# Attention back stage: a step's small products moved from its end to mid-step

## The chip, the cores and the metric

The kernel runs on one core of one Trainium2 chip. The metric is the device time of one execution in microseconds. Three runs of the kernel before gave 2210.7, 2211.61 and 2214.48 us; the median is 2211.61 us.

## What is computed

The input x is 16 batches of 512 tokens of 128 values in f32. The reference chains six blocks:

```python
x = x + 0.5 * _L0_ffn_ref(_layernorm(x), ...)   # 16 experts, top 2, and a shared one
x = x + _L0_attn_ref(_layernorm(x), ...)         # linear attention
x = x + 0.5 * _L0_ffn_ref(_layernorm(x), ...)
x = x + 0.5 * _L1_ffn_ref(_layernorm(x), ...)    # relu MLP of width 512
x = x + _L1_attn_ref(_layernorm(x), ...)         # softmax attention, 16 heads of 8
x = x + 0.5 * _L1_ffn_ref(_layernorm(x), ...)
```

The last two are the part of this case:

```python
# _L1_attn_ref
xn = _layernorm(x, ln_scale, ln_bias)
q, k, v = xn @ wq, xn @ wk, xn @ wv              # each split into 16 heads of 8
scores = jnp.einsum('bhid,bhjd->bhij', q, k)
probs = jax.nn.softmax(scores / jnp.sqrt(128.0), axis=-1)
out = jnp.einsum('bhij,bhjd->bhid', probs, v)    # heads joined again
return out + xn
# _L1_ffn_ref
h = jax.nn.relu(x @ w1 + b1)
return h @ w2 + b2
```

## The kernel before

The program has two stages, one after the other. The front (`build_front`) does the first four blocks and writes its result to the DRAM tensor `mid`. The back (`build_back`, from L882) does the last two. The change touches the back alone. In the notes below PE is the matrix engine, DVE the vector engine, ACT the scalar engine, POOL and SP the two others.

**Batches and steps.** The back has 16 batches. A batch has 16 steps k: 4 groups g of 4 heads, and in each group 4 blocks of 128 keys (`STEPS = GRP * T`). Every engine runs its own `batch_steps(B)` once for each batch, with its own written order of instructions; semaphores tie the orders together. The program is written out for batches -2 to 16, and what does not exist is left out.

**What a step does.** A step has four units j, one for each head of the group.
- `scores` (L1404) writes the transposed scores of a key block and 512 queries, 128x512, into an ST bank. ACT takes the exponential (L1184) into `pr`. Below such a tile is called ST0 to ST3.
- `first_scores` (L1417) writes 128 queries by 512 keys into an MX bank, 7 steps ahead (`AHEAD`). DVE takes the maximum of each row (L1302) into `nm`. These are MX0 to MX3. After four steps the maxima of a group are transposed (`nm`, L1379), copied with the sign changed by ACT (L1168), and sent by SP (L1049) into an extra row of `qt`, from where they shift the scores.
- `weighted` (L1432) multiplies the exponentials of the step before with the values into the bank PV. It waits for all four exponentials of that step (L1425). It is called PV below.

**The order on PE in a step** (L1436 to L1447) is ST0, MX0, ST1, MX1, PV of the step before, ST2, MX2, ST3, MX3, and at the end the small products of that step. The scores use 32 rows of the array each, and the four units sit on four different groups of rows.

**Small products.** The table `SMALL` (L856) gives each step its list. Its names: `xt` transposes the normalised input of the next batch; `kp`, `qp` and `v` are the projections to keys, queries and values; `nm` the transposed maxima; `ot` the transposed output of a group; `ft` transposes the input of the MLP; `g` are four products into the hidden layer, and `y` its two output products. Three engines follow the list:
- PE makes the product into a bank.
- ACT handles `v` and `g` and `nm` (`FOR_ACT` and `nm`). For `xt`, `kp`, `qp`, `ft` (`BY_BOTH`) ACT copies the high part and then DVE subtracts it for the low part (L1230 to L1239).
- DVE handles `ot` and `y`.

**Rings.** PSUM has 8 banks: 3 for ST, 4 for MX, one for PV. `ST_RING` and `MX_RING` (L871 to L877) list all that goes into these banks in PE's order; an entry's place modulo the number of banks is its bank. `v` and `g` are in the ST ring, all others in the MX ring. `wait_bank` (L1335) makes PE wait until the entry that had the bank before has been used. The ST ring has 69 places, the MX ring 78, and both start anew with every batch.

**Orders of the others.** ACT: exponentials 0 and 1, then every fourth step the copy of PV (L1190), exponentials 2 and 3, then the small ones. DVE: maximum 0, then the low parts of the step before, maximum 1, then `side` (statistics of the layer norms), maxima 2 and 3, then `ot` and `y`. SP issues the transfers in the order of L1052 to L1074, POOL the normalisations in the order of L1105 to L1133. They wait on the semaphores `khi_ready`, `used["kp"]`, `used["nm"]`, `used["ot"]`, `used["y"]` and the like.

Of the kernel before, what the change touches and what calls it, by code (L numbers as in the profile page):

```python
# [36 lines left out]
HG = H // GRP  # L37
# [69 lines left out]
def build_front(nc, weights, x_dram, mid_dram, ident_dram, turns):  # L107
# [748 lines left out]
SMALL = [  # L856
# [4 lines left out]
FOR_ACT = ("v", "g")  # L861
BY_BOTH = ("xt", "kp", "qp", "ft")
# [3 lines left out]
def ahead_of(k):  # L866

    return (0, k + AHEAD) if k + AHEAD < STEPS else (1, k + AHEAD - STEPS)


ST_RING, MX_RING = [], []  # L871
for _k, _small in enumerate(SMALL):
    _rel, _s = ahead_of(_k)
    ST_RING += [("st", 0, _k * HG + _j) for _j in range(HG)] + [one for one in _small if one[0] in FOR_ACT]
    MX_RING += [("mx", _rel, _s * HG + _j) for _j in range(HG)] + [one for one in _small if one[0] not in FOR_ACT]
ST_PLACE = {one: _p for _p, one in enumerate(ST_RING)}
MX_PLACE = {one: _p for _p, one in enumerate(MX_RING)}  # L877

# [3 lines left out]
def build_back(nc, weights, mid_dram, out_dram, staged_dram, tail_dram, batches):  # L882
    w = weights
    with ExitStack() as ctx:
# [97 lines left out]
        def first_head(u):  # L982

            return (u + HG // 2) % HG
# [5 lines left out]
        def bank_of(name, rel, n):  # L990
            if name in FOR_ACT:
                return ST[ST_PLACE[name, rel, n] % ST_BANKS]
            return MX[MX_PLACE[name, rel, n] % MX_BANKS]

        def program(batch_steps):


            for n in range(-2, batches + 1):
                batch_steps(Batch(n // 2, n % 2))
# [143 lines left out]
        @block.scalar  # L1143
        def _(act):
            def small(B, rel, name, n):
                C = B + rel
                if not C.exists or name not in IN_ACT:
                    return
                p = C.parity
                act.wait_ge(made[name].sem, C.at(made[name], n + 1))  # L1150
                m = bank_of(name, rel, n)
                if name == "xt":
                    nc.scalar.activation(xh[:], m[:], ACT.Copy).then_inc(xh_ready.sem, 1)
                elif name == "kp":
                    if not C.first:
                        act.wait_ge(staged.sem, C.at(staged, 0))
                    nc.scalar.activation(khi[:], m[:], ACT.Copy).then_inc(khi_ready.sem, 1)
                elif name == "qp":
                    if not C.first:
                        act.wait_ge(staged.sem, C.at(staged, 0))  # L1160
                    nc.scalar.activation(qhi[:], m[:], ACT.Copy).then_inc(qhi_ready.sem, 1)
                elif name == "ft":
                    nc.scalar.activation(fh[:], m[:], ACT.Copy).then_inc(fh_ready.sem, 1)
                elif name == "nm":
                    if n >= 2 or not C.first:
                        before = (C, n - 2) if n >= 2 else (C + -1, n + GRP - 2)
                        act.wait_ge(shift_in[before[1]].sem, before[0].at(shift_in[before[1]], 16 * T))
                    nc.scalar.activation(nr[n % 2][:], m[0:32, 0], ACT.Copy, scale=-1.0).then_inc(used["nm"].sem, 1)  # L1168
                elif name == "v":
                    nc.scalar.activation(va[p][:, :, :, 0:DH], m[:].rearrange("p t (h e) -> p t h e", h=H),  # L1170
                                         ACT.Copy).then_inc(used["v"].sem, 1)
                elif name == "g":
                    nc.scalar.activation(hid[n][:], m[:], ACT.Relu, bias=w["b1"][:, n:n + 1]).then_inc(used["g"].sem, 1)

            def exponential(B, k, j):
                if not B.exists:
                    return
                u = k * HG + j
                act.wait_ge(made["st"].sem, B.at(made["st"], u + 1))
                if j == 0 and (k >= 2 or not B.first):  # L1180

                    act.wait_ge(pv_mm.sem, B.at(pv_mm, k - 1))
                bank = ST[ST_PLACE["st", 0, u] % ST_BANKS]
                nc.scalar.activation(pr[k % 2][:, j], bank[:].rearrange("p a b -> p (a b)"),  # L1184
                                     ACT.Exp, scale=SM_SCALE).then_inc(used["st"].sem, 1)

            def weights_out(B, g):
                if B.exists:
                    act.wait_ge(pv_mm.sem, B.at(pv_mm, T * (g + 1)))
                    nc.scalar.activation(oTs[g % 2][:], PV[:], ACT.Copy).then_inc(pv_out.sem, 1)  # L1190

            def batch_steps(B):
                for k in range(STEPS):
                    for j in range(HG):
                        exponential(B, k, j)
                        if j == 1 and k == 0:
                            weights_out(B + -1, GRP - 1)
                        elif j == 1 and k % T == 0:
                            weights_out(B, k // T - 1)
                    for name, rel, n in SMALL[k]:  # L1200
                        small(B, rel, name, n)

            program(batch_steps)

        @block.vector
        def _(dve):
# [83 lines left out]
            def maximum(B, rel, u):  # L1290

                C = B + rel
                if not C.exists:
                    return
                g, t, j = u // (HG * T), u // HG % T, first_head(u)
                dve.wait_ge(made["mx"].sem, C.at(made["mx"], u + 1))
                if u % (HG * T) == 0 and (g >= 2 or not C.first):
                    before = (C, g - 1) if g >= 2 else (C + -1, g + GRP - 1)
                    dve.wait_ge(made["nm"].sem, before[0].at(made["nm"], before[1]))
                c = t * HG + j  # L1300
                bank = MX[MX_PLACE["mx", rel, u] % MX_BANKS]
                nc.vector.tensor_reduce(nm[g % 2][:, c:c + 1], bank[:].rearrange("p a b -> p (a b)"), AX.X,  # L1302
                                        ALU.max).then_inc(used["mx"].sem, 1)

            def batch_steps(B):
                for k in range(STEPS):
                    rel, s = ahead_of(k)
                    maximum(B, rel, s * HG)
                    for name, r, n in SMALL[k - 1]:
                        if name in BY_BOTH:  # L1310
                            small(B, r, name, n)
                    maximum(B, rel, s * HG + 1)
                    side(B, k)
                    maximum(B, rel, s * HG + 2)
                    maximum(B, rel, s * HG + 3)
                    for name, r, n in SMALL[k]:
                        if name not in IN_ACT:
                            small(B, r, name, n)

            for k in range(2):  # L1320
                own.step(nc.vector.memset(nm[k][:], 0.0))
            own.settle()
            program(batch_steps)

        @block.tensor
        def _(pe):
# [68 lines left out]
            def scores(B, k, j):  # L1395

                if not B.exists:
                    return
                g, u = k // T, k * HG + j
                if k % T == 0 and j == 0:  # L1400
                    pe.wait_ge(shift_in[g].sem, B.at(shift_in[g], 16 * T))
                place = ST_PLACE["st", 0, u]
                wait_bank(B, ST_RING, ST_BANKS, place)
                pe.matmul(flat(ST[place % ST_BANKS]), kt_[g][rows_of(j), k % T], flat(qt[g])[rows_of(j)], start=True,  # L1404
                          stop=True).then_inc(made["st"].sem, 1)
# [30 lines left out]
            def batch_steps(B):  # L1436
                for k in range(STEPS):
                    rel, s = ahead_of(k)
                    for j in range(HG):
                        scores(B, k, j)  # L1440
                        first_scores(B, rel, s * HG + j)
                        if j == 1 and k == 0:
                            weighted(B + -1, STEPS - 1)
                        elif j == 1:
                            weighted(B, k - 1)
                    for name, r, n in SMALL[k]:
                        small(B, r, name, n)  # L1447

            program(batch_steps)

# [254 lines left out]
```

## Time and profile before

| | |
|---|---|
| median of three runs | 2211.61 us |
| profiled execution, device time | 2212.05 us |
| its span | 2210.3 us |
| mean granted clock of PE | 0.969 |
| busy in the span: PE | 1984.1 us (90%) |
| DVE | 1650.0 us (75%) |
| ACT | 1083.3 us (49%) |
| POOL | 585.6 us (26%) |

The profiled execution stands 0.44 us from the median. In the page's view of 40 slices the back begins at about slice 24 and fills the rest. The engine PEld in the rows is the loading of weights into PE, which overlaps its products. Ends of matmuls are modelled, so the starts are what is read. In the timeline view instructions of one kind that follow each other are merged, with their number after x; the time given is from the first start to the last end. Four score products of different row groups run side by side, so that four starts lie within 0.01 us.

### The profile page before, as it was taken

Reading aid. Unit: us, or ns where it says so; the run is one execution under the profiler, and the core shown is the slowest. Engines: PE = TensorE matmul, PEld = TensorE weight load, DVE = VectorE, ACT = ScalarE, POOL = GpSimd, SP = SyncE. Lnnn points to the kernel's source line nnn. Section 1 sums busy time; section 2 is a strip of 40 time slices with the busy share of each in tenths; the row PEclk is TensorE's granted clock in tenths of the full one; section 3 lists DMA queues with packets and bytes.
Section 4 is the critical chain, followed back from the end, with each engine's and each line's share of the span. In section 5 each row is a group of like instructions: output and inputs, shape, how many; then the busy total and the mean of one; then the engine's idle time right before and its main releaser. Section 6 shows DMA issues by size and latency. Waiting matters only on the chain. (4 is left out here: it accounts for less than half of the span.)

```text
span 2210.3 us, 34280 instructions
## 1 busy us (share of the span) xinstructions
PE 1984.1 (90%) x12468; PEld 1352.9 (61%) x12468; DVE 1650.0 (75%) x4096; ACT 1083.3 (49%) x1971; POOL 585.6 (26%) x621
## 2 busy tenths in 40 slices
PE   3998999899989998989899838999999999999997
PEld 3787778777877787778777723344444444444444
DVE  5766776767676767776767518988988888889982
ACT  3333323332333233323332214777777777777775
POOL 3332333233223331333133021222222222222211
PEclk9999999999999999999999956999999999999999
DMA  3000000000000000000000022222222222222220
GB/s 119 6 11 10 1 11 10 11 1 10 11 10 1 10 11 10 1 11 11 10 1 6 5 72 81 73 81 84 78 78 78 78 87 88 78 78 78 73 73 10
DMA packets 49991, 85.81 MB, mean 39 GB/s; under 512 B 6752, under 2 KB 11104, under 8 KB 49760
## 3 DMA queue, kind: packets, MB, share of 16 engines
q1 hardware_dynamic: 47920, 81.85, 11.6%
q8 instruction: 99, 1.62, 0.3%
q10 hardware_dynamic: 1904, 1.78, 0.2%
q14 instruction: 68, 0.56, 0.1%
HBM read 49.26 MB, written 34.87 MB: 38 GB/s over the span
## 5 line engine op out<-in xcount | busy, mean ns | idle before, releaser
L1302 DVE TENSOR_REDUCE b_nm<-b_MX 128x1 f32<-128x512 f32 x1024 | 651.8, 683 | 80.1 <-PE b_MX L1417 71.4
L1184 ACT ACTIVATE b_pr<-b_ST 128x512 f32<-128x512 f32 x1024 | 551.7, 601 | 175.8 <-PE b_ST L1404 173.9
L383 ACT ACTIVATE s<-G 128x512 f32<-128x512 f32 x306 | 182.9, 598 | 432.3 <-PE G L685 423.2
L1417 PE MATMUL b_MX<-b_kt,b_qt 32*128 32x512 f32 x1024 | 357.7, 505 | 20.8 <-DMA b_qt<-staging 8.3
L690 PE MATMUL Y<-w_wd,h 128*128 128x128 f32 x2448 | 335.0, 281 | 8.6 <-DVE h L544 8.0
L690 PEld LDWEIGHTS Y<-w_wd,h 128*128 128x128 f32 x2448 | 315.0, 195 | 23.9 <-DVE h L544 13.4
L1404 PE MATMUL b_ST<-b_qt,b_kt 32*128 32x512 f32 x1024 | 305.8, 497 | 19.5 <-ACT b_pr L1184 18.7
L1404 PEld LDWEIGHTS b_ST<-b_qt,b_kt 32*128 32x128 f32 x1024 | 123.3, 183 | 317.0 <-ACT b_pr L1184 214.4
L535 DVE TENSOR_TENSOR su<-U,s 128x512 f32<-128x512 f32 x272 | 186.3, 685 | 160.8 <-ACT s L383 83.1
L1432 PE MATMUL b_PV<-b_pr,b_va 128*32 128x512 f32 x2048 | 276.2, 612 | 0.0
L544 DVE TENSOR_TENSOR h<-C,su 128x512 f32<-128x512 f32 x272 | 188.1, 692 | 9.3
L1417 PEld LDWEIGHTS b_MX<-b_kt,b_qt 32*128 32x128 f32 x1024 | 142.9, 186 | 60.7 <-DVE b_nm L1302 34.0
L683 PE MATMUL U<-xh,w_wuh 128*128 128x512 f32 x306 | 128.3, 419 | 57.6 <-DVE su L535 44.0
L305 POOL TENSOR_TENSOR vpe_s<-mv_s,w_eps 128x4 f32<-128x4 f32 x33 | 6.6, 199 | 627.0 <-DVE mv_s L437 627.0
L683 PE MATMUL G<-xh,w_wgh 128*128 128x512 f32 x306 | 145.6, 476 | 0.0
L1098 POOL TENSOR_TENSOR b_ve<-b_mv,w_eps_two 128x4 f32<-128x4 f32 x16 | 3.2, 201 | 445.9 <-DVE b_mv L1219 445.9
L685 PE MATMUL G<-xl,w_wgh 128*128 128x512 f32 x306 | 121.3, 396 | 0.0
L685 PE MATMUL U<-xl,w_wuh 128*128 128x512 f32 x306 | 121.2, 396 | 0.0
L684 PE MATMUL G<-xh,w_wgl 128*128 128x512 f32 x306 | 120.9, 395 | 0.0
L684 PE MATMUL U<-xh,w_wul 128*128 128x512 f32 x306 | 120.8, 395 | 0.0
L683 PEld LDWEIGHTS U<-xh,w_wuh 128*128 128x128 f32 x306 | 57.7, 189 | 97.0 <-DVE su L535 58.8
L718 PE MATMUL C<-cT,w_pairs 128*128 128x512 f32 x272 | 109.1, 401 | 0.0
(237 smaller groups left out, 3431.9 us busy)
## 6 DMA issues: line engine op xcount, KB each, us to landing
b_kt<-staging SPq DMA_DIRECT2D x64, 256.0 KB, 2.8
b_qt<-staging SPq DMA_DIRECT2D x64, 256.0 KB, 3.1
staging<-b_khi SPq DMA_DIRECT2D x32, 256.0 KB, 3.0
staging<-b_qhi SPq DMA_DIRECT2D x32, 256.0 KB, 3.0
xin<-in_x SPq DMA_DIRECT2D x17, 256.0 KB, 2.6
mid<-xo SPq DMA_DIRECT2D x17, 256.0 KB, 2.0
b_x<-mid SPq DMA_DIRECT2D x16, 256.0 KB, 2.9
staging<-b_klo SPq DMA_DIRECT2D x16, 256.0 KB, 3.1
```

What stands on the lines that cost most here:

```text
L383: nc.scalar.activation(sbuf_s[n % 2][:], G[n % 2][:], ACT.Silu).then_inc(act_done.sem, 1)
L535: nc.vector.tensor_tensor(out[:], U[:], sbuf_s[n % 2][:], ALU.mult).then_inc(up_used.sem, 1)
L544: nc.vector.tensor_tensor(h[n % 3][:], C[:], su[n % 2][:], ALU.mult).then_inc(h_ready.sem, 1)
L683: pe.matmul(flat(bank), wh, flat(high), start=True, stop=False)
L684: pe.matmul(flat(bank), wl, flat(high), start=False, stop=False)
L685: return pe.matmul(flat(bank), wh, flat(low), start=False, stop=True)
L690: mm = pe.matmul(bank[:, t], hid[:, t], wd, start=(first and t == 0), stop=True, skip_group_check=True)
L1184: nc.scalar.activation(pr[k % 2][:, j], bank[:].rearrange("p a b -> p (a b)"), ACT.Exp, scale=SM_SCALE).then_inc(used["st"].sem, 1)
L1302: nc.vector.tensor_reduce(nm[g % 2][:, c:c + 1], bank[:].rearrange("p a b -> p (a b)"), AX.X, ALU.max).then_inc(used["mx"].sem, 1)
L1404: pe.matmul(flat(ST[place % ST_BANKS]), kt_[g][rows_of(j), k % T], flat(qt[g])[rows_of(j)], start=True, stop=True).then_inc(made["st"].sem, 1)
L1417: pe.matmul(flat(MX[place % MX_BANKS]), qt[g][rows_of(j), u // HG % T], flat(kt_[g])[rows_of(j)], start=True, stop=True).then_inc(made["mx ...
L1432: mm = pe.matmul(flat(PV)[rows_of(j)], va[B.parity][:, kt, g * HG + j], pr[k % 2][:, j], start=(kt == 0), stop=(kt == T - 1), skip_group_c ...
```

## The change

In the two rings, the small products of a step get their places after unit 1 and before unit 2 (before: after unit 3). PE issues them directly behind PV, between unit 1 and unit 2. ACT handles its own after exponential 1 (and the copy of PV, where there is one). DVE does `ot` and `y` between `side` and maximum 2, and the low parts of the same step between maximum 2 and maximum 3 (before: in the next step, after maximum 0). SP's and POOL's programs are unchanged.

```diff
 for _k, _small in enumerate(SMALL):
     _rel, _s = ahead_of(_k)
-    ST_RING += [("st", 0, _k * HG + _j) for _j in range(HG)] + [one for one in _small if one[0] in FOR_ACT]
-    MX_RING += [("mx", _rel, _s * HG + _j) for _j in range(HG)] + [one for one in _small if one[0] not in FOR_ACT]
+    for _half in (range(0, 2), range(2, HG)):
+        ST_RING += [("st", 0, _k * HG + _j) for _j in _half]
+        MX_RING += [("mx", _rel, _s * HG + _j) for _j in _half]
+        if 0 in _half:
+            ST_RING += [one for one in _small if one[0] in FOR_ACT]
+            MX_RING += [one for one in _small if one[0] not in FOR_ACT]
...
 # ACT, batch_steps
-                    for name, rel, n in SMALL[k]:
-                        small(B, rel, name, n)
+                        if j == 1:
+                            for name, rel, n in SMALL[k]:
+                                small(B, rel, name, n)
...
 # DVE, batch_steps
                     maximum(B, rel, s * HG)
-                    for name, r, n in SMALL[k - 1]:
-                        if name in BY_BOTH:
-                            small(B, r, name, n)
                     maximum(B, rel, s * HG + 1)
                     side(B, k)
-                    maximum(B, rel, s * HG + 2)
-                    maximum(B, rel, s * HG + 3)
                     for name, r, n in SMALL[k]:
                         if name not in IN_ACT:
                             small(B, r, name, n)
+                    maximum(B, rel, s * HG + 2)
+                    for name, r, n in SMALL[k]:
+                        if name in BY_BOTH:
+                            small(B, r, name, n)
+                    maximum(B, rel, s * HG + 3)
...
 # PE, batch_steps
-                    for name, r, n in SMALL[k]:
-                        small(B, r, name, n)
+                        if j == 1:
+                            for name, r, n in SMALL[k]:
+                                small(B, r, name, n)
```

## Rows read from the trace of the kernel before

**Rows 1.** Windows view: start:end, length, busy and count by engine, PEclk, DMA, GB/s.
```profile
1716.63:1769.02 52.39, 51.06 (x347) 22.81 (x346) 47.12 (x97) 40.71 (x82) 13.13 (x15) 1.00 0.25 82
1716.00:1725.40 9.40, 8.23 (x58) 2.84 (x55) 7.98 (x15) 6.97 (x15) 6.73 (x6) 1.00 0.34 114
```
**Rows 2.** Waits view, the same batch: who waited for whom, us, times, longest.
```profile
PEld b_ST L1404 <- ACT b_pr L1184: 12.9, 19, 1.0
...
ACT b_pr L1184 <- PE b_ST L1404: 11.6, 15, 1.7
```
**Rows 3.** Timeline, step 2 (no small product): start, length, engine, line, operation, count.
```profile
1723.73 0.49 PE L1404 MATMUL b_ST<-b_qt,b_kt 32*128 32x512 f32 x1
...
1724.26 2.06 ACT L1184 ACTIVATE b_pr<-b_ST 128x512 f32<-128x512 f32 x4 [1.15 <-PE b_ST L1404]
1724.30 2.48 DVE L1302 TENSOR_REDUCE b_nm<-b_MX 128x1 f32<-128x512 f32 x4 [0.36 <-PE b_MX L1417]
...
1724.91 0.50 PE L1404 MATMUL b_ST<-b_qt,b_kt 32*128 32x512 f32 x1 [0.45 <-ACT b_pr L1184]
...
1725.40 1.07 PE L1432 MATMUL b_PV<-b_pr,b_va 128*32 128x512 f32 x8
```
**Rows 4.** Timeline, step 10 (one product g) and the start of step 11.
```profile
1748.90 0.49 PE L1404 MATMUL b_ST<-b_qt,b_kt 32*128 32x512 f32 x1
...
1749.33 0.50 PE L1331 MATMUL b_ST<-b_fh,w_w1h 128*128 128x512 f32 x1
...
1750.23 0.49 PE L1404 MATMUL b_ST<-b_qt,b_kt 32*128 32x512 f32 x1
...
1750.39 0.69 ACT L1173 ACTIVATE b_hid<-b_ST,w_b 128x512 f32<-128x512 f32 x1
...
1750.96 1.10 ACT L1184 ACTIVATE b_pr<-b_ST 128x512 f32<-128x512 f32 x2
1750.99 1.06 PE L1432 MATMUL b_PV<-b_pr,b_va 128*32 128x512 f32 x8
```
**Rows 5.** Timeline, step 3 (xt) with the start of step 4; and MX1, PV of step 6.
```profile
1726.83 0.66 PE L1365 MATMUL b_MX<-w_ident,b_xn 128*128 128x128 f32 x4
...
1727.42 0.50 PE L1404 MATMUL b_ST<-b_qt,b_kt 32*128 32x512 f32 x1
...
1727.90 0.61 ACT L1153 ACTIVATE b_xh<-b_MX 128x512 fp32r<-128x512 f32 x1
...
1728.38 1.11 ACT L1184 ACTIVATE b_pr<-b_ST 128x512 f32<-128x512 f32 x2
1728.88 0.68 DVE L1230 TENSOR_TENSOR b_xl<-b_MX,b_xh 128x512 fp32r<-128x512 f32 x1
...
1735.06 0.50 PE L1417 MATMUL b_MX<-b_kt,b_qt 32*128 32x512 f32 x1
1735.48 1.06 PE L1432 MATMUL b_PV<-b_pr,b_va 128*32 128x512 f32 x8
1736.48 0.50 PE L1404 MATMUL b_ST<-b_qt,b_kt 32*128 32x512 f32 x1
```
**Rows 6.** Timeline, PE: nm and qp, v, ot and y, y; each with what follows.
```profile
1733.41 0.28 PE L1379 MATMUL b_MX<-w_ident,b_nm 128*32 128x128 f32 x1
...
1734.49 0.49 PE L1404 MATMUL b_ST<-b_qt,b_kt 32*128 32x512 f32 x1
...
1739.65 0.33 PE L1373 MATMUL b_ST<-w_wvh,b_xh 128*128 128x128 f32 x1
...
1741.14 0.49 PE L1404 MATMUL b_ST<-b_qt,b_kt 32*128 32x512 f32 x1
...
1761.80 0.66 PE L1383 MATMUL b_MX<-w_ident,b_oTs 128*128 128x128 f32 x4
...
1764.17 0.50 PE L1404 MATMUL b_ST<-b_qt,b_kt 32*128 32x512 f32 x1
...
1766.04 2.05 PE L1388 MATMUL b_MX<-w_w,b_hid 128*128 128x128 f32 x16
...
1768.02 0.50 PE L1404 MATMUL b_ST<-b_qt,b_kt 32*128 32x512 f32 x1
```

## Prediction

> **What bounds the kernel now.** The front is untouched, so only the back matters: 16 batches of 16 steps. The time from one batch to the next is 52.40 us: the windows view of one batch runs from one values' product to the same one a batch later [rows 1]. In it PE is busy 51.06 us, DVE 47.12, ACT 40.71 [rows 1]. The reader should see that PE looks full, and then open the waits [rows 2]: the exponentials wait 11.6 us a batch for scores on PE, and PE's next score load waits 12.9 us for exponentials. The two pass work to each other through three banks.
>
> The timeline shows how the hand-over works. Call t the moment at which the group ST2, MX2, ST3, MX3 starts. Step 2 has no small product [rows 3]: t is 1723.73, the two exponentials of ST2 and ST3 start at 1724.26 (0.53 later; the four take 2.06 us, so 0.49 apart, with 0.60 for the last), and the next values' product starts at 1725.40. It needs all four exponentials of its step (L1425): 0.53 + 0.49 + 0.60 + 0.04 = 1.66, against a measured 1.67. So between t and the values' product PE owes 1.66 us to ACT, however little PE has to do. Its own work there is two groups of score products, 0.43 each. What is left is idle: the second group shows 0.45 us of waiting for the exponential.
>
> Step 10 has a product g behind its group [rows 4]: g starts at 1749.33 and the next scores at 1750.23, so it takes 0.90 us of PE. The whole link from t (1748.90) to the values' product (1750.99) is 2.09 us, only 0.43 more than without g. About half of g ran while ACT worked through ST2 and ST3. That shadow is what the present place gives, to most of the small products.
>
> **The change, part by part.** No instruction is added or removed. PE's order in a step goes from ST0 MX0 ST1 MX1 PV ST2 MX2 ST3 MX3 small to ST0 MX0 ST1 MX1 PV small ST2 MX2 ST3 MX3. A step from PV to PV is then PV (1.00 us from its start to the next start [rows 5]), the small product s, and a link L from t to the next PV, in which no small product stands. The time of a step is 1.00 + s + L.
>
> *The small products.* Transposes of a 128x512 tile (xt, ft, ot in step 6) 0.59 us each (1726.83 to 1727.42 [rows 5]): 1.77. nm and qp together 1.08 [rows 6]; a product alone is 0.90, so nm ahead of something costs about 0.17: nm + ot in steps 1 and 9 0.76 each, 1.52. kp and four g, 0.90 each: 4.50 (the nm beside the last g taken as nothing, as it overlaps). v 1.49, ot + y 2.37, y 1.98 [rows 6]. Sum 14.71 us. On PE they cost the same at either place.
>
> *The link L, by kind of step.*
> - No ACT work for the small product (steps 0, 1, 2, 6, 9, 14; nm's copy of 32 partitions is made before ST2 is ready): L = 1.66 [rows 3]. Six steps: 9.96. In step 0 the copy of PV may add 0.1; left out.
> - v or g (steps 7, 10 to 13): made at about t + 0.1, its ACT instruction goes ahead of the exponential, as the order says. It takes 0.57 to the next start (1750.39 to 1750.96 [rows 4]), so the exponential starts at 0.68 instead of 0.53: L = 1.81. The tile taken by g is the one that ST0 of the next step needs, free at about t + 0.85: early enough. Five steps: 9.05.
> - xt, kp, qp, ft (steps 3, 4, 5, 8). Here the rings matter. With four MX banks and the small product now two places earlier, MX1 of the next step takes the very bank of the small product, and waits until DVE has subtracted the low part. Before, that bank went to MX3 of the next step, much later. DVE's order is now maximum 2, low part, maximum 3. From t: maximum 2 starts at 0.57 (1723.73 to 1724.30 [rows 3]), the low part 0.60 later (four maxima take 2.48, so 0.60 apart [rows 3]) and takes 0.68 [rows 5], then 0.04 to PE, and 0.42 from MX1 to the values' product (1735.06 to 1735.48 [rows 5]): 0.57 + 0.60 + 0.68 + 0.04 + 0.42 = 2.31. ACT's high part (ready at about 0.71) is in time. Queued behind the waiting MX1 on PE are the values' product, the next small product and the next scores; everybody waits. Four steps: 9.24.
> - Step 15: MX has 78 places over 4 banks, which leaves a remainder of two, so at the wrap MX1 of step 0 takes the bank of MX3 of step 15, one maximum after MX2: again 2.31. Before it took y's bank.
>
> Sum of L: 9.96 + 9.05 + 9.24 + 2.31 = 30.56. A batch: 16.00 + 14.71 + 30.56 = 61.27 us, against 52.40: +8.87. The first batch lacks what belongs to its predecessor (ot, ft, g, y), the last what belongs to its successor (xt, kp, qp, v and most maxima); together they hold about one set, so 15 batches: +133 us. The profiled execution took 2212.05 us (span 2210.3; the median of the runs is 2211.61, 0.4 below): 2212.05 + 133 = **2345 us**.
>
> *Covers and queues at nothing.* DVE has 61.27 us for 47.12 of work; at t it has been through maxima 0 and 1 and the side work (MX1 is issued 0.42 before PV, two maxima take 0.60 + 0.68 and at most two short statistics follow, while PV and a small product take 1.59 or more), so it is not late for maximum 2. In steps with ot or y it does these ahead of maximum 2, within or just after the 0.57. nm needs the last maximum of the step before: done at t + 1.9, the transpose stands at t + 2.66 at the earliest. SP: the shift of a group, issued on nm's copy, and the staging on the high and low parts move up by half a step in a longer batch; nothing on SP gets later than its user. POOL: its input statistics and ot keep their places, its results have half a step less and 17% more time per step. Each of these is nothing, and if one cover were missing it would add to the loss (one more wait of a maximum is 0.6 us a batch, 9 us in all).
>
> **Bounds.** Below: if the low-part and wrap waits did not bind (slack on DVE or PE that I don't see), step 15's link falls to 1.66 and the other four to 1.73 (ACT's high part goes first and takes 0.48 to the next start, 1727.90 to 1728.38 by the second exponential's row [rows 5], so the exponential starts at 0.60): 0.65 + 4 x 0.58 = 2.97 us a batch, 45 in all. Above: the small product behind PV is a pair of shapes that the trace of before does not show, and an exponential may start a little later than 0.53. I allow 0.12 a step for both, an estimate (three hand-overs of 0.04): 16 x 15 x 0.12 = 29 us. What a half-drained queue gives back at the new place can't be seen here; between the ends I take the rows as they stand.
>
> **Rivals.**
> 1. *Only the exponentials bind* (the lower bound). For it: ring waits of today are small. Against: the order of DVE is fixed and its low part stands behind maximum 2. 2345 - 45 = 2300. Chance 0.12.
> 2. *Faster: the halves balance and DVE becomes the bound.* Today PE waits for y's addition in step 15 and for maxima and low parts here and there; with the small product in mid-step ACT and DVE have it and PV to catch up, and results come half a step earlier. If all PE waits vanished, the batch would be DVE's 47.12 us: 5.28 less, -79 over 15, 2133. It decides at a link of (52.40 - 14.71 - 16.00) / 16 = 1.36 us on average: below it the change gains. Steps without a small product show 1.66 [rows 3], and nothing in the change shortens two exponentials in a row. Chance 0.03.
> 3. *Nothing moves* (the order was not what set the step): 2212. The 0.43 instead of 0.90 that g costs today speaks against it. Chance 0.02.
> 4. *The clock falls.* PE would be idle some 15% of a batch in place of 2.5%. Steps 0 to 2 are already 8.23 of 9.40 us busy at a granted clock of 1.00, the 2.4 GHz level [rows 1], and no stretch in the steady back shows less. If a tenth of the back ran at 1.2 GHz, PE's own 44 us a batch (16 x 1.86 + 14.71) would grow by 4.4, +66 us: 2411. Chance 0.04.
>
> The Trainium skill has a rule that speaks for rival 4: in "TensorE: Matmul & The Clock Gate", section "A second HAM failure mode: psum-queue depth-cycling", it says that a kernel which goes round its PSUM banks and leaves PE idle for a moment between groups can see the clock swing between its two levels. By that rule the time would be the 2411 above, or more. The trace does not bear it out so far: with idle gaps of 0.4 to 0.5 us in steps 0 to 2 the clock stays at 1.00.
>
> **Chances and range.** My forecast 0.79, the rivals 0.12, 0.03, 0.02, 0.04. The range takes in rival 1 and the upper bound: 2297 to 2376. Slower by over 0.2% (4.4 us, about what a measurement of this kernel can tell from no change): 0.95; within it 0.02; faster 0.03. The sign rests on one thing: the values' product waits for the last exponential, and the work that filled that wait is moved in front of it.
>
> **What the profile after would show.** A batch of 61.3 us instead of 52.4. In step 10: PV, then g 1.00 us later, ST2 0.90 after that, and 1.8 us to the next PV, with PE idle in between. In the waits: PE for exponentials at PV grows from almost nothing to some 5 us a batch; a new wait of MX1 for the low part, in steps 4, 5, 6 and 9, of 1 us or more; one for maximum 3 in step 0. ACT and DVE idle longer, waiting for PE. PE busy at about 85% at a clock of 1.00. I am wrong if steps 3, 4, 5, 8 have a link near 1.7 (rival 1), if links are below 1.4 (rival 2), or if the clock row of the back shows less than 1.00 (rival 4).

## The result, and the profile after

The changed kernel takes 2349.27 us (median of four runs, 2344.7 to 2361.47) against 2212.18 us for the kernel before, measured beside it. The ratio is 1.0624, with a 95% interval from 1.0600 to 1.0648: 137 us slower. The forecast was 2345 us, slower.

The page of the profiled execution (2352.97 us, span 2350.9) shows where: busy time hardly changes, the waits do. These are its first part and the first three groups of its part 5 (line, engine, operation, tiles, count; busy time and mean ns; idle time before them and its releaser).

```profile
PE 2026.9 (86%) x12468; PEld 1350.4 (57%) x12468; DVE 1650.2 (70%) x4096; ACT 1089.5 (46%) x1971; POOL 586.2 (25%) x621
...
L1307 DVE TENSOR_REDUCE b_nm<-b_MX 128x1 f32<-128x512 f32 x1024 | 641.6, 683 | 169.2 <-PE b_MX L1422 165.9
L1188 ACT ACTIVATE b_pr<-b_ST 128x512 f32<-128x512 f32 x1024 | 527.8, 605 | 154.7 <-PE b_ST L1409 154.5
L1409 PE MATMUL b_ST<-b_qt,b_kt 32*128 32x512 f32 x1024 | 335.8, 484 | 104.4 <-ACT b_pr L1188 77.4
```

DVE waited 80.1 us for its maxima before and waits 169.2 now; PE's score products waited 19.5 us and wait 104.4. DVE does the same 1650 us of work. Nobody became the bound. The engines wait for each other more.

The windows view of one batch, from one copy of PV to the same copy a batch later, answers to [rows 1]; the two others are the stretch behind step 8 of one batch and the stretch behind step 5 of the next, and will be needed further down (start:end, length, busy and count of PE, PEld, DVE, ACT, POOL, then PEclk, DMA share, GB/s).

```profile
2087.76:2148.83 61.07, 53.08 (x350) 22.34 (x352) 47.17 (x96) 41.10 (x82) 13.15 (x15) 1.00 0.22 69
1807.60:1812.50 4.90, 4.44 (x26) 1.70 (x25) 2.97 (x7) 1.74 (x5) 0.00 (x0) 0.65 0.02 5
1858.80:1863.60 4.80, 4.35 (x21) 1.56 (x20) 2.96 (x7) 1.45 (x4) 2.24 (x2) 0.64 0.66 195
```

A batch is 61.07 us where the forecast had 61.27 and before it was 52.40. DVE and ACT do in it what they did [rows 1: 47.12 and 40.71], to a tenth on DVE and 0.4 on ACT. The waits view of the same 61.07 us, us in total, times, longest:

```profile
PEld b_ST L1409 <- ACT b_pr L1188: 13.0, 18, 1.0
...
DVE b_nm L1307 <- PE b_MX L1422: 9.6, 10, 1.6
...
PE b_ST L1409 <- ACT b_pr L1188: 4.8, 10, 0.5
PEld b_PV L1437 <- ACT b_pr L1188: 4.6, 16, 0.3
```

PEld before PV waits in all 16 steps, 4.6 us in sum, and the view names an exponential each time; the kernel before shows 1.6 us in 6 of them. In 11 steps that is the hand-over of which the forecast said that it would bind. In the other five (behind xt, kp, qp, ft and y with the wrap) the forecast had MX1 come last, and step 3 below shows it: the exponential that PV needs has ended when MX1 starts, and PV follows MX1 by 0.42.

**Step 10, with a product g** (timeline: start, length, engine, line, operation, count, idle before). It answers to [rows 4].

```profile
1812.47 1.06 PE L1437 MATMUL b_PV<-b_pr,b_va 128*32 128x512 f32 x8
1813.47 0.51 PE L1336 MATMUL b_ST<-b_fh,w_w1h 128*128 128x512 f32 x1
...
1814.37 0.50 PE L1409 MATMUL b_ST<-b_qt,b_kt 32*128 32x512 f32 x1
...
1814.48 0.69 ACT L1177 ACTIVATE b_hid<-b_ST,w_b 128x512 f32<-128x512 f32 x1 [1.07 <-PE b_ST L1338]
...
1815.22 0.50 PE L1409 MATMUL b_ST<-b_qt,b_kt 32*128 32x512 f32 x1 [0.35 <-ACT b_hid L1177]
...
1816.19 1.06 PE L1437 MATMUL b_PV<-b_pr,b_va 128*32 128x512 f32 x8
```

g starts 1.00 after PV and takes 0.90; t is 1814.37 and the next PV comes 1.82 later. The step takes 3.72 us; before it took 3.09. Note the row of ACT L1177: ACT has been idle for 1.07 us when g is at last made. ACT and PE take turns.

**Step 3, with xt**, answers to [rows 5]:

```profile
1848.02 0.49 PE L1409 MATMUL b_ST<-b_qt,b_kt 32*128 32x512 f32 x1
...
1848.59 0.69 DVE L1307 TENSOR_REDUCE b_nm<-b_MX 128x1 f32<-128x512 f32 x1 [0.37 <-PE b_MX L1422]
1848.62 2.06 ACT L1188 ACTIVATE b_pr<-b_ST 128x512 f32<-128x512 f32 x4
1849.19 0.68 DVE L1235 TENSOR_TENSOR b_xl<-b_MX,b_xh 128x512 fp32r<-128x512 f32 x1
...
1849.93 0.49 PE L1422 MATMUL b_MX<-b_kt,b_qt 32*128 32x512 f32 x1 [0.16 <-DVE b_xl L1235]
1850.35 1.07 PE L1437 MATMUL b_PV<-b_pr,b_va 128*32 128x512 f32 x8
```

t is 1848.02. Maximum 2 starts at t + 0.57, the low part at 1.17 and ends at 1.85, MX1 starts at 1.91 and PV at 2.33: the chain of the forecast (2.31), link by link. The last exponential of step 3 ends at about 1849.7 (two of the four in the row of ACT), so it is not what PV waits for. The wait shows only 0.16 of idle time at MX1, as ST0, MX0 and ST1 ran inside it; the row with the longest idle time is not the one that sets the time here.

### The profile page after: what moved, and what is told of

It is laid out like the page before. It is cut to its first block and busy times, and to the rows that moved or that the text cites. A ratio compares the mean times of both kernels' runs of the same rounds, so it can differ in the third digit from the quotient of the medians.

```text
span 2350.9 us, 34282 instructions
## 1 busy us (share of the span) xinstructions
PE 2026.9 (86%) x12468; PEld 1350.4 (57%) x12468; DVE 1650.2 (70%) x4096; ACT 1089.5 (46%) x1971; POOL 586.2 (25%) x621
## 5 line engine op out<-in xcount | busy, mean ns | idle before, releaser
L1307 DVE TENSOR_REDUCE b_nm<-b_MX 128x1 f32<-128x512 f32 x1024 | 641.6, 683 | 169.2 <-PE b_MX L1422 165.9
L1188 ACT ACTIVATE b_pr<-b_ST 128x512 f32<-128x512 f32 x1024 | 527.8, 605 | 154.7 <-PE b_ST L1409 154.5
L1409 PE MATMUL b_ST<-b_qt,b_kt 32*128 32x512 f32 x1024 | 335.8, 484 | 104.4 <-ACT b_pr L1188 77.4
L1422 PE MATMUL b_MX<-b_kt,b_qt 32*128 32x512 f32 x1024 | 342.0, 494 | 31.8 <-DVE b_nm L1307 12.4
L1409 PEld LDWEIGHTS b_ST<-b_qt,b_kt 32*128 32x128 f32 x1024 | 130.5, 186 | 304.8 <-ACT b_pr L1188 200.1
L1437 PE MATMUL b_PV<-b_pr,b_va 128*32 128x512 f32 x2048 | 282.5, 624 | 1.2 <-ACT b_pr L1188 1.2
L1422 PEld LDWEIGHTS b_MX<-b_kt,b_qt 32*128 32x128 f32 x1024 | 133.3, 189 | 70.8 <-DVE b_nm L1307 32.5
```

Source lines behind the costliest of these rows:

```text
L1422: pe.matmul(flat(MX[place % MX_BANKS]), qt[g][rows_of(j), u // HG % T], flat(kt_[g])[rows_of(j)], start=True, stop=True).then_inc(made["mx ...
L1437: mm = pe.matmul(flat(PV)[rows_of(j)], va[B.parity][:, kt, g * HG + j], pr[k % 2][:, j], start=(kt == 0), stop=(kt == T - 1), skip_group_c ...
```

## The experiments

All of them are made from the kernel before or the changed one; the batch lengths are from one copy of PV to the same a batch later, in a stretch without a drop of the clock (below). Each ratio is to the kernel before measured beside the run: 2211.99 us for the runs with four kinds put back, with these four alone and with g thinned, 2211.75 us for v and g and for nm, ot and y, 2214.54 us for the other four. The changed kernel's 2349.27 us stands beside 2212.18, so a difference to it carries a few microseconds of doubt. What is said of the clock rests on one trace of each kernel.

### xt, kp, qp and ft put back to the end

```diff
+MID = ('nm', 'ot', 'v', 'g', 'y')
...
-        if 0 in _half:
-            ST_RING += [one for one in _small if one[0] in FOR_ACT]
-            MX_RING += [one for one in _small if one[0] not in FOR_ACT]
+        _now = at_mid(_k) if 0 in _half else at_end(_k)
+        ST_RING += [one for one in _now if one[0] in FOR_ACT]
+        MX_RING += [one for one in _now if one[0] not in FOR_ACT]
...
```

The rest of the edit does the same on PE, ACT and DVE: what `MID` names stands in mid-step, the rest at the end, with DVE's low parts after maximum 0 of the next step, as before. The next three kernels differ from this one in `MID` alone.

> The changed kernel with xt, kp, qp and ft (the products whose bank DVE needs for the low part) put back to the end of their steps, in the rings and in all orders; nm, ot, v, g and y stay in mid-step. Theory (link and ring): steps 3, 4, 5 and 8 go back to about their old 2.84, 3.38, 3.86 and 2.76 us from 3.91, 4.22, 4.25 and 3.92 now, 3.4 us a batch, about 50 us in all, and the drops of the clock behind the long waits of MX1 vanish with them (some 7 of 1.5 us in the profiled execution): 2285 to 2300 us. Rival (every small product costs its own PE time wherever it loses its cover, the ring plays no part): these four are 3.0 of 14.7 us of small products, so a fifth of the loss, 2320 us, and the clock drops stay.

Measured 2289.26 us (2280.29 to 2296.91), ratio 1.0341 (1.0311 to 1.0371): 60 us less than the changed kernel. A batch takes 57.34 us, 3.73 less; 3.4 was expected. So these four, a fifth of the small work, carry over 3 of the 8.7 us that a batch loses. Steps 3, 4 and 8 went back to 2.85, 3.37 and 2.76 us, but step 5 went to 3.30 and not to its old 3.85: with nm in mid-step and qp at the end it is shorter than in either kernel. Why is open. But the clock drops did not vanish. In this profiled execution there are seven values' products of 1.93 or 1.94 us, one in step 8 of every second batch, behind the product v. So the drops are not tied to the long waits of MX1 alone, as the theory had it. The windows view over one of them:

```profile
1600.98:1604.98 4.00, 4.00 (x23) 1.40 (x21) 2.59 (x5) 2.83 (x6) 0.00 (x0) 0.57 0.47 157
```

### xt, kp, qp and ft alone in mid-step

```diff
+MID = ('xt', 'kp', 'qp', 'ft')
```

> The kernel before with xt, kp, qp and ft alone in mid-step, everything else at the end. Theory (link and ring): it loses what the run with these four put back regains, 50 us plus the clock drops: 2262 to 2275 us, and the clock drops appear behind the waits of MX1 in steps 5 to 6 and 8 to 9. Rival (share by PE time): 2212 + 28 = 2240 us, with no drop of the clock.

Measured 2275.36 us (2269.93 to 2276.1), ratio 1.0273 (1.0255 to 1.0291): +63 us. A batch without a drop takes 55.62 us, 3.2 more than before: 48 us over 15 batches. The rest goes by the trace to drops of the clock. Seven long values' products stand alone, two in step 4, two in step 5 and three in step 9, behind waits of MX1 as the theory had it, and four stand in a row from 1405.81 us, at the turn of the first two batches. None is in step 8: v is at the end here.

### v and g alone, and nm, ot and y alone

The one kernel:

```diff
+MID = ('v', 'g')
```

The other:

```diff
+MID = ('nm', 'ot', 'y')
```

> The kernel before with v and g alone (the small products of the ST ring) in mid-step, the rest at the end. Theory (each kind of small product adds the difference of its steps, read from the two traces): step 7 goes from 3.36 to 4.21 us, steps 10 to 13 from 3.09, 3.10, 3.19, 3.08 to 3.72, 3.72, 3.72, 3.74: 3.29 us a batch, 49 in all, 2261 us, plus what clock drops add (0 to 12 us). Theory on the clock (a step of v in mid-step is enough for a drop behind it, as with only xt, kp, qp, ft put back): long values' products in step 8 appear here as well. Rival (the kinds share one loss, and it is mostly due to the MX ring): under 20 us, below 2232 us, no drops.

> The kernel before with nm, ot and y alone in mid-step. Theory (sum over steps): step 6 +0.51, step 14 +0.79, step 15 +0.88, steps 1, 9 and 13 about nothing: 2.2 us a batch, 33 in all, 2245 us; with the 63 us of xt, kp, qp, ft alone and the 49 of v and g the three parts then make up the 137 us of the whole change to within 15 us. Rival (y in mid-step costs its full 3.8 us a batch, as all its cover is lost): 57 us, 2269 us. No drop of the clock expected, as v and the low parts stay where they were.

v and g: 2266.16 us (2262.88 to 2270.18), ratio 1.0244 (1.0220 to 1.0268), +54 us. A batch is 55.64 us, 3.25 more, with 3.29 read from the steps of the two traces; four long values' products of 1.93 us stand in step 8 of every second batch of the later half, as was expected here. nm, ot and y: 2237.11 us (2236.31 to 2239.0), ratio 1.0111 (1.0090 to 1.0131), +25 us. Its batch is 54.26 us, 1.87 more (28 us over 15 batches); 2.2 was expected. No drop of the clock. It also has a term that was not expected: step 5 fell from 3.85 to 3.29 us, as its nm left the end. The three parts make 63 + 54 + 25 = 142 us, the whole change 137, each with its own drops of the clock. By the batches alone it is 3.2 + 3.25 + 1.87 = 8.3 us against 8.68. So the loss is close to a sum over kinds of small products, step by step, and not one effect of the new order. The sum fails most in step 5, where qp alone adds 0.38 us, nm alone takes 0.56 off and both together add 0.40.

### g thinned, at the end and in mid-step

```diff
-                    mm = product(m, w["w1h"][:, n], w["w1l"][:, n], fh, fl)
+                    mm = pe.matmul(flat(m), w["w1h"][:, n], flat(fh), start=True, stop=True)
```

> The kernel before with each product g made of one matmul in place of three (the two correction terms of the MLP's first layer are left out), 0.47 us of PE less in steps 10 to 13. Theory A (the ring sets the link there): ST1 of the next step takes the bank of ST3 and waits for its exponential whatever g takes, so the link stays at 2.09 us and the time at 2212, within 4 us. Theory B (the prediction's reading: half of g lies on PE's path): 0.43 us less in each of four steps, 26 us in all, 2186 us.

> The changed kernel with the same one matmul in place of three in each g (the two correction terms left out). Both theories: in mid-step nothing covers g, so its whole 0.47 us come off in four steps of 15 batches, 28 us, 2321 us. Rival (the loss comes from another wait, and PE has slack at g too): no change, 2349 us.

At the end of the step: 2210.9 us (2209.04 to 2216.16), ratio 0.9995 (0.9985 to 1.0004). Two thirds of the matmuls of g are gone and the time is the same. In mid-step: 2321.66 us (2319.8 to 2322.88), ratio 1.0489 (1.0473 to 1.0504), 28 us less than the changed kernel, as expected. Step 10 falls from 3.72 to 3.25 us, by 0.47, and a batch from 61.07 to 59.29. This is the cleanest statement of what the change does: at the end of steps 10 to 13 those 0.47 us of PE cost nothing, in mid-step they cost all they take. The timeline of step 10 with g thinned at the end:

```profile
1747.49 1.06 PE L1432 MATMUL b_PV<-b_pr,b_va 128*32 128x512 f32 x8
1748.49 0.49 PE L1404 MATMUL b_ST<-b_qt,b_kt 32*128 32x512 f32 x1
...
1749.02 1.09 ACT L1184 ACTIVATE b_pr<-b_ST 128x512 f32<-128x512 f32 x2 [0.94 <-PE b_ST L1404]
...
1750.16 0.49 PE L1404 MATMUL b_ST<-b_qt,b_kt 32*128 32x512 f32 x1
...
1750.59 1.07 PE L1432 MATMUL b_PV<-b_pr,b_va 128*32 128x512 f32 x8
```

From PV to PV it is 3.10 us, as with the whole g (3.09). The two exponentials end at 1750.11, ST1 starts at 1750.16 and PV 0.43 behind it. With one place more in the ST ring, ST1 of the next step takes the bank of ST3 and waits for its exponential. That, and not g's time on PE, makes the link 2.10 us. The kernel before, with the whole g, has the same hand-over in step 10: the two exponentials end at 1750.50 and ST1 starts at 1750.56.

```profile
1749.42 1.08 ACT L1184 ACTIVATE b_pr<-b_ST 128x512 f32<-128x512 f32 x2 [0.94 <-PE b_ST L1404]
...
1750.56 0.50 PE L1404 MATMUL b_ST<-b_qt,b_kt 32*128 32x512 f32 x1
```

### The low part ahead of maximum 2

```diff
-                    maximum(B, rel, s * HG + 2)
                     for name, r, n in SMALL[k]:
                         if name in BY_BOTH:
                             small(B, r, name, n)
+                    maximum(B, rel, s * HG + 2)
                     maximum(B, rel, s * HG + 3)
```

> The changed kernel with DVE's low part put ahead of maximum 2 instead of behind it. Theory (MX1 of the next step waits for the low part by the ring): the low part starts when ACT's high part is ready, about 0.75 us after t, MX1 gets its bank at 1.47 instead of 1.89, the link of steps 3, 4, 5, 8 falls from 2.31 to about 1.9, 0.4 x 4 x 15 = 24 us less, and the clock drops become fewer: 2312 to 2325 us. Rival (these links are long for another reason, such as ACT's high part ahead of the exponentials): no change, 2343 to 2349 us.

Measured 2315.43 us (2314.82 to 2316.27), ratio 1.0468 (1.0448 to 1.0489): 34 us less than the changed kernel, with nothing but the order of two instructions on DVE changed in four steps. A batch is 59.38 us, 1.69 less (1.6 expected), 25 us in all; step 3 fell from 3.91 to 3.49 us. The rest goes by the traces to the clock, as one long values' product stands in this one and eight in that of the changed kernel. The ring wait was real, and DVE's order set its length.

### More work for PE inside the wait

```diff
                 wait_bank(B, ST_RING, ST_BANKS, place)
+                for _ in range(2 if j == 1 and k in (4, 5, 6, 9) else 0):
+                    pe.matmul(flat(ST[place % ST_BANKS]), kt_[g][rows_of(j), k % T], flat(qt[g])[rows_of(j)],
+                              start=True, stop=True)
```

> The changed kernel with the score matmul ST1 of steps 4, 5, 6 and 9 issued three times in a row into the same bank (the same result, 0.43 us more of PE work, inside PE's wait for the low part, which lasts longer than that). Theory (the drops of the clock come from PE's idle time in the run of long waits): the drops behind steps 5 and 8 vanish, the granted clock of the back is 1.00 throughout, the batch stays at 61.07 us, and the time falls by the drops, 5 to 12 us, to 2337 to 2344 us, with less spread between runs. Rival (the drops are independent of that idle time, or the added work lands on the path): as many drops, 2349 us, or up to 0.43 x 4 x 15 = 26 us more.

Measured 2342.64 us (2342.12 to 2346.37), ratio 1.0595 (1.0572 to 1.0617), against 2349.27, and the spread of four runs shrinks from 16.8 to 4.3 us. The two medians were not measured side by side and their ratios to the kernel before overlap in their intervals, so I rest on the traces: two long values' products in place of eight, and from the first to the last copy of PV 953.6 us in place of 962.6. Nine microseconds for six drops is 1.5 us each. A batch without a drop takes 61.07 us as before: the 128 or so redundant matmuls made the kernel no slower. The five drops in steps 5, 6 and 9, where or just behind where the work was added, are gone. Two remain in step 8, behind v, where none was added; the theory had these vanish too.

### Two ways to use the end of a step better

The first moves `ot` of group 2 from step 14 to step 0 of the next batch:

```diff
-    [], [("nm", 0, 1), ("ot", -1, 3)], [], [("xt", 1, 0)],
+    [("ot", -1, 2)], [("nm", 0, 1), ("ot", -1, 3)], [], [("xt", 1, 0)],
...
-    [("g", -1, 2)], [("nm", 1, 0), ("g", -1, 3)], [("ot", 0, 2), ("y", -1, 0)], [("y", -1, 1)]]
+    [("g", -1, 2)], [("nm", 1, 0), ("g", -1, 3)], [("y", -1, 0)], [("y", -1, 1)]]
```

> The kernel before with one small product moved: ot of group 2 goes from step 14 (beside a y) to step 0 of the next batch, which has none; still at the step's end. Theory (the end of a step hides about one transpose of a tile, and step 14 has long overrun its cover): step 14 falls from 4.25 to about 3.7 us, step 0 stays near 2.8: 7 us less, 2205 us. Rival (DVE or the ring takes it back, as ot costs DVE 0.57 us wherever it stands): 2212 us, within 4 us.

Measured 2208.43 us (2203.16 to 2212.47), ratio 0.9974 (0.9959 to 0.9989). A batch is 52.11 us, 0.3 less, 4 us over 15 batches: step 14 fell from 4.25 to 3.85 us, step 1 rose from 3.34 to 3.45. The direction holds. By the batch the size is somewhat over half of the 7 us expected; the medians, 2214.54 and 2208.43, lie 6 us apart.

The second cuts `y` into four (the main lines; DVE's addition is cut in the same way, the program runs one batch further, and SP stores a batch after step 2 of the next but one):

```diff
-    [], [("nm", 0, 1), ("ot", -1, 3)], [], [("xt", 1, 0)],
+    [("y", -2, 2)], [("nm", 0, 1), ("ot", -1, 3)], [("y", -2, 3)], [("xt", 1, 0)],
...
-                    half = slice(2 * n, 2 * n + 2)
+                    half = slice(n, n + 1)
...
-                    for t in range(2):
+                    for t in range(1):
                         for f in range(FT):
-                            mm = pe.matmul(m[:, t], hid[f][:, 2 * n + t], w["w2"][:, f], start=(f == 0),
+                            mm = pe.matmul(m[:, t], hid[f][:, n], w["w2"][:, f], start=(f == 0),
```

> The kernel before with y in four quarters at the ends of steps 14, 15, 0 and 2 in place of two halves at 14 and 15 (the last two in the next batch, the store of a batch after step 2). Theory (each step's end hides small work up to its cover, so spread it): steps 14, 15, 0, 2 take about 3.4, 3.1, 3.1, 3.1 us in place of 4.25, 4.42, 2.77, 2.66, 1.4 us less a batch, 21 us, 2191 us. Rival (DVE is the next bound: two more instructions a batch and no slack in steps 0 to 2): 2205 to 2215 us.

Measured 2184.75 us (2182.6 to 2190.36), ratio 0.9881 (0.9857 to 0.9905): 1.2% faster than the kernel before, and the fastest of the study; 30 us less where 21 were expected. Steps 14, 15, 0 and 2 take 3.35, 2.96, 2.96 and 2.95 us, 12.2 in place of 14.1. A stretch of 50.50 us, about one batch, and the start of step 15 in the timeline, with a quarter of y:

```profile
1700.00:1750.50 50.50, 50.23 (x348) 22.53 (x347) 47.15 (x99) 40.88 (x82) 13.15 (x14) 1.00 0.27 85
```

```profile
1707.74 1.06 PE L1433 MATMUL b_PV<-b_pr,b_va 128*32 128x512 f32 x8
...
1709.17 1.16 PE L1389 MATMUL b_MX<-w_w,b_hid 128*128 128x128 f32 x8
...
1710.26 0.50 PE L1405 MATMUL b_ST<-b_qt,b_kt 32*128 32x512 f32 x1
...
1710.70 1.06 PE L1433 MATMUL b_PV<-b_pr,b_va 128*32 128x512 f32 x8
```

The quarter takes 1.09 us of PE (1709.17 to 1710.26) and adds only 0.3 to the 2.66 us of a step without a small product. DVE is now busy for 47.15 of 50.50 us.

## Why the prediction was right, point by point

*The link.* "The values' product waits for the last exponential, and the work that filled that wait is moved in front of it" is what the trace after shows, in each kind of step but those where a ring wait comes later still. The forecast's steps stand beside those of one undisturbed batch: no small product 2.66 (measured 2.66), step 0 2.66 (2.76, by the copy of PV that I left out), xt 3.90 (3.91), kp 4.21 (4.23), nm and qp 4.39 (4.25), v 4.30 (4.21), ft 3.90 (3.92), nm and ot 3.42 (3.32), g 3.71 (3.72), ot and y 5.03 (5.04), y with the wrap 5.29 (5.30). The worst is nm + qp: its nm ran beside the product and cost nothing, as it did beside g. For v the forecast took g's 0.57 us from ACT's copy to the next exponential, and v's takes 0.50. No experiment made the exponentials shorter; that they set the 1.66 rests on the traces and on g in mid-step, where PE's time comes off in full.

*The ring.* The bank of the small product as the new place for MX1 was read from the ring's list alone, without a row of before that showed such a wait. Turning DVE's order (1.69 us a batch) confirms it, and putting the four back (3.73 us) agrees. Rival 1, "only the exponentials bind", was refuted: the link of step 3 is 2.33 us and not 1.73. The forecast had MX1 waiting 1 us or more, though. The rows show PE idle for 0.16 to 0.18 us before it and PEld for 0.5, as other scores run inside the wait; the end of the chain was right, the idle time was not.

*What was wrong in the reading of before.* "About half of g ran while ACT worked through ST2 and ST3" is not how it was. The whole of g was hidden; the 0.43 us that a step with g costs over one without comes from ST1's wait for the bank of ST3, a matter of places in a ring of three. The thin g at the end (ratio 0.9995) decides against the half. By the same chain it would be there for a g of no length, which no run shows. The forecast did not suffer, since it used g's full length and a new link, neither of which rests on that sentence. It would have misled whoever had set out to shorten g.

*The clock.* The forecast had the clock at 1.00, and its own sign of being wrong by rival 4, less than 1.00 in the back, came: the rival had 0.04 and came true in part. Between the first batch and the last copy of PV the clock fell eight times for a few microseconds; the mean granted clock of the two stretches shown above is 0.65 and 0.64. This is step 6 of one batch, with t of step 5 at 1856.49:

```profile
1858.41 0.49 PE L1422 MATMUL b_MX<-b_kt,b_qt 32*128 32x512 f32 x1 [0.18 <-DVE b_qlo L1241]
...
1858.83 1.87 PE L1437 MATMUL b_PV<-b_pr,b_va 128*32 128x512 f32 x8
...
1860.63 1.12 PE L1388 MATMUL b_MX<-w_ident,b_oTs 128*128 128x128 f32 x4
...
1861.68 0.79 PE L1409 MATMUL b_ST<-b_qt,b_kt 32*128 32x512 f32 x1
```

PV takes 1.80 us to the next start in place of 1.00 and the transposes 1.05 in place of 0.59: the 1.2 GHz level, in between 2.4 before and after. Such a batch is 62.6 us long, with two of them 64.2. Eight times 1.5 us is 12 us, far below the 66 us of the rival. The Trainium skill's section that was weighed in the prediction ("TensorE: Matmul & The Clock Gate", "A second HAM failure mode: psum-queue depth-cycling") reports such swings of the clock for another kernel, which goes round its PSUM banks and leaves PE idle often and briefly. This case's trace agrees in what is seen: no idle row of PE around that stretch is longer than 0.51 us, and the clock falls. That going round the banks is the cause no run here shows; the kernel before goes round the same banks, with 0.45 us of idle time in step 2 [rows 3], at 1.00.

*The sum.* From the first to the last copy of PV the back takes 962.6 us after and 822.0 before, 141 more. Some 12 of them are the clock, so the order itself cost 128 where 133 was forecast. The steps listed above make 3 of these 5 us, nm beside qp and ot, and v, against the copy of PV left out; the rest is not traced. So a sum of the order a little too large and a clock term put at nothing met at 137: that the forecast came within 4 us of the median is luck in part, and the mechanism is right to about 5 of 133 us. (The stated range reached 3 and 2 us further than the two bounds that it was built from, 2300 and 2374.) Part of the difference between runs lies ahead of the back: the first copy of PV stands between 1360.0 and 1367.0 us in the traces of this study (1364.4 before, 1364.1 after).

## What to carry to other kernels

When two engines hand tiles back and forth through few banks, each order has a stretch in which one must wait whatever it does; the step with the least work shows its length (2.66 us here, for 1.86 of PE work). Work put into that stretch cost little here: a quarter of y, 1.09 us of PE, cost 0.3, xt of 0.59 cost 0.2, and a g 0.43 whether it was 0.90 or 0.43 long, by its place in the ring. The same g in mid-step cost its full time and 0.16 more. So spread small work in pieces over such stretches rather than gather it (y in quarters: 1.2% faster). And when an item moves in a ring, list who takes its bank next: the new neighbour waits for its last reader, and where that reader stands in its engine's order can be worth more than the item (two lines on DVE: 25 us).

## What the runs showed of the hardware that was not expected

PE's clock fell from its 2.4 GHz level to 1.2 with no idle row longer than about half a microsecond around it. The changed kernel keeps PE busy for 53.08 of 61.07 us and has eight such drops; none of the steady back of the kernel before (51.06 of 52.39) shows one. The share of idle time alone does not tell which kernel has them. These are a batch of the kernel with v and g alone in mid-step, which has four drops, and one of the kernel with nm, ot and y alone, which has none and leaves PE idle for a larger share:

```profile
1905.78:1961.40 55.62, 52.67 (x350) 23.23 (x352) 46.66 (x96) 40.80 (x81) 13.12 (x15) 1.00 0.24 77
1724.76:1779.00 54.24, 50.89 (x350) 22.41 (x352) 47.21 (x96) 40.82 (x81) 13.15 (x15) 1.00 0.25 80
```

In the changed kernel the eight slow values' products are two in step 5, one in step 6, three in step 8 and two in step 9, behind the long waits of MX1 or behind v. With more PE work in the waits there were two in place of eight, with the shorter waits one, and all three of these stand in step 8. With g thinned in mid-step there were eight again, in steps 4, 5 and 9 and none in step 8. But with the long waits gone there were seven, all behind v, each 116.05 us after the last, two batches; with v and g alone four, 112.66 us apart, again two batches. That such a drop comes in the same step of every second batch, and not in the batches between, is not explained by the work of the step, which is the same in each.

The start of the back is another matter: each kernel has slow values' products there, the kernel before four, from 1349 to 1363 us, and in the profiled run of y in quarters the granted clock is also 0.50 from 1385.5 to 1402.6 us, though nothing was moved to mid-step. What decides when the clock falls stays open.
